# First attention of a two-layer transformer: the projections read raw transposed rows instead of rows that were normalized and transposed on the chip

## The reference, cut to what matters

```python
def _layernorm(x, axis=-1, eps=1e-05):
    m = jnp.mean(x, axis=axis, keepdims=True)
    v = jnp.var(x, axis=axis, keepdims=True)
    return (x - m) / jnp.sqrt(v + eps)
...
x = L0_attn_x                                   # 8 x 512 x 128
x = x + _L0_attn_ref(_layernorm(x), Wq, Wk, Wv, g_scale)
...
q = (x @ Wq.T)   # of the normalized rows; k and v in the same way
q, k = q / |q|, k / |k|  per head;  softmax(g_scale * q k^T) v
```

## Time and profile before

| what | us |
|---|---|
| timed runs: median of 3 (lowest to highest) | 1465.96 (1461.98 to 1473.85) |
| the profiled execution, its own time | 1452.33 |
| its span from first to last instruction | 1450.6 |
| busy in that span: PE / DVE / ACT / POOL | 1281.0 / 952.6 / 858.0 / 607.1 |
| mean granted clock of TensorE, of full speed | 0.960 |

### The profile page before, as it was taken

The page is one execution under the profiler, slowest core; times in us unless marked ns, Lnnn a source line. Parts: engine busy times, 40 slices in busy tenths (PEclk is TensorE's granted clock), DMA queues, the critical chain, the costliest instruction groups (busy, mean ns, idle before and its releaser), DMA issues.

```text
span 1450.6 us, 28493 instructions
## 1 busy us (share of the span) xinstructions
PE 1281.0 (88%) x9302; PEld 790.0 (54%) x9302; DVE 952.6 (66%) x3308; ACT 858.0 (59%) x1679; POOL 607.1 (42%) x783
## 2 busy tenths in 40 slices
PE   3877899999999999999999999998888886989982
PEld 1223455555555555555555555555555554878872
DVE  4475665677677766767676776656665762776784
ACT  3766666676666766675666676654534542555563
POOL 1000133342444435442533453345435444657674
PEclk8979999999999999999999999999989998999996
DMA  8041290000000000000000000001010001142422
GB/s 339 1 187 71 9 5 1 1 9 1 8 9 16 8 2 16 8 9 1 23 2 8 7 11 1 8 9 66 8 73 16 1 8 41 53 115 70 129 65 92
DMA packets 65455, 54.68 MB, mean 38 GB/s; under 512 B 41016, under 2 KB 51648, under 8 KB 65056
## 3 DMA queue, kind: packets, MB, share of 16 engines
q1 hardware_dynamic: 60768, 43.48, 14.0%
q0 software_dynamic: 4544, 9.38, 1.9%
HBM read 21.03 MB, written 31.81 MB: 36 GB/s over the span
## 4 chain that ended last, share of the span: by engine, by line
PE 61%; DVE 17%; ACT 10%; issue 7%; POOL 2%; POOLq 1%; DMA 0%; ACTq 0%; SPq 0%; DVEq 0%
PE scores L1745 11%; PE outs L1763 9%; PE outs L1889 7%; PE work L1685 7%; PE work L1792 4%; DVE scores L1238 3%; PE scores L1876 3%; DVE ra L1231 3%; ACT a_buf L947 3%; ACT ra L953 3%; PE outs L1968 2%; PE scores L1714 2%; PE work L1692 2%; PE work L1851 1%; PE work L1802 1%
## 5 line engine op out<-in xcount | busy, mean ns | idle before, releaser
L1238 DVE CUSTOM_DVE_ANT_0 scores<-scores,mask_qk 128x512 f32<-128x512 f32 (+3 forms) x512 | 238.8, 518 | 148.7 <-PE scores L1714 148.7
L941 ACT ACTIVATE big<-scores 128x1024 f32<-128x1024 f32 (+1 forms) x192 | 169.8, 885 | 214.3 <-PE scores L1745 214.2
L786 POOL TENSOR_SCALAR_AFFINE_SELECT big<-big 128x256 f32<-128x256 f32 x256 | 101.6, 410 | 461.0 <-ACT big L941 436.3
L947 ACT ACTIVATE a_buf<-scores 128x1024 f32<-128x1024 f32 x256 | 248.0, 1028 | 44.1 <-PE scores L1876 43.9
L1745 PE MATMUL scores<-ra 64*128 64x512 f32 (+3 forms) x1536 | 184.1, 345 | 10.6 <-ACT a_buf L947 4.7
L806 POOL TENSOR_TENSOR big<-big 128x768 f32<-128x768 f32 x64 | 116.8, 1824 | 136.2 <-issue 53.3
L1763 PE MATMUL outs<-big 128*64 128x512 f32 (+3 forms) x1024 | 156.9, 450 | 0.0
L1745 PEld LDWEIGHTS scores<-ra 64*128 64x128 f32 x1536 | 121.5, 187 | 61.7 <-issue 41.5
L1231 DVE TENSOR_TENSOR ra<-work,ra 128x512 fp32r<-128x512 f32 x128 | 88.3, 690 | 89.4 <-ACT ra L953 89.4
L1889 PE MATMUL outs<-a_buf 128*16 128x512 f32 x1024 | 143.8, 637 | 1.5 <-ACT a_buf L947 1.4
L1022 ACT ACTIVATE big<-scores,b_sb 128x128 f32<-128x128 f32 x312 | 89.4, 370 | 76.2 <-PE scores L1956 75.2
(11 more groups left out here) (223 smaller groups left out, 2540.5 us busy)
## 6 DMA issues: line engine op xcount, KB each, us to landing
sorted_rows<-xrows SPq DMA_DIRECT2D x34, 520.0 KB, 6.9
qkT<-sorted_rows SPq DMA_DIRECT2D x78, 65.0 KB, 1.8
a_buf<-in_w SPq DMA_DIRECT2D x2, 2048.0 KB, 7.9
a_buf<-in_x SPq DMA_DIRECT2D x8, 256.0 KB, 2.7
x_rows<-x SPq DMA_DIRECT2D x8, 256.0 KB, 2.0
ra<-x_rows SPq DMA_DIRECT2D x8, 256.0 KB
a_buf<-choice_rows SPq DMA_DIRECT2D x6, 256.0 KB, 3.9
yT<-choice_rows SPq DMA_DIRECT2D x5, 256.0 KB, 2.7
```

The costliest lines, as they stand in the source:

```text
L941: activation(prob1(g, i), d[:, :, 0:256] if i == 2 else d, ACT.Exp, scale=SCALE1).then_inc(unit_free("pair", g, i), 1)
L947: activation(prob0(c)[:, i * 1024:(i + 1) * 1024], unit_wait(act, "cosine", c, i), ACT.Exp).then_inc(unit_free("cosine", c, i), 1)
L1238: return v.tensor_tensor_reduce(scores_, scores_, mask_qk[:, SEQ - width:SEQ], -1.0, 3e38, ALU.add, ALU.min, neg_max[:, qt, j:j + 1])
```

## The change

The host hands over a second copy of the input, `x_T0`, with each batch transposed (128 numbers by 512 rows). SP loads it straight into `xT_h`, batch after batch, with one DMA of 256 KB each, which waits until the projections of the batch before were issued to the end. The standardizing instructions, the transposes, their copy, and the buffer `rows_h` go away, and POOL's wait for `rows_ready["a0"]` at `p = 3` with them.

The mean of a row is taken out by the weights: with W the weights by input, `(x - mean(x)) W = x (W - column mean of W)`. Once, at the start, PE sums the columns of the three weights with a matrix of ones (two matmuls, one for each half of the partitions of a bank), and DVE adds -1/128 of the sums to the weights. The factor `rstd` of a row, which is a row of the projection's result too, is applied by ACT when it moves the result: the two copies per tile become two activations that read a scale for each partition. The variances stay where they were, and use the second slot of their small buffers.

```diff
@@ work_order
     if p == 4:
         add(f, ("y0", f, 0), ("y0", f, 1))
-        add(h, ("xT0", h))
@@ SP
+            def next_x_T(h):
+                if h:
+                    work_wait(sp, "qkv0", h - 1, TILES - 1)
+                sp.dma_start(xT_h, x_T0[h]).then_inc(x_T_loaded, 16)
+
             sp.dma_start(x_in(0), x[0]).then_inc(x_loaded[0], 16)
             for dst, src in ((wqkv0_sb[:], wqkv0), (g_sb[:], g_scale.to_broadcast([P, 1]))):
                 sp.dma_start(dst, src).then_inc(first_in, 16)
+            next_x_T(0)
...
             for n in range(FILLS // 2):
                 zero_fill(n)
 
+            next_x_T(1)
+
             def next_x(h):
                 sp.wait_ge(x_taken, h - 1)
                 sp.dma_start(x_in(h), x[h]).then_inc(x_loaded[h % 2], 16)
+                next_x_T(h)
@@ POOL
-                if p == 3 and h is not None:
-                    pool.wait_ge(rows_ready["a0"], h + 1)
...
-                    inverse_deviations("a0", h)
+                    inverse_deviations("a0", h, 1)
@@ ACT
                 w = work_wait(act, "qkv0", h, t)
-                copy(qk0(h).rearrange("p (w t n) -> p w t n", w=2, t=TILES)[:, :, t, :],
-                     w[:, 0:2 * DIM].rearrange("p (w n) -> p w n", w=2))
-                copy(vstat(h)[:, t, :, 0:D0],
-                     w[:, 2 * DIM:3 * DIM].rearrange("p (h d) -> p h d", d=D0)
-                     ).then_inc(free_of("qkv0", h, t), 1)
+                act.wait_ge(rstd_ready["a0"], h + 1)
+                activation(qk0(h).rearrange("p (w t n) -> p w t n", w=2, t=TILES)[:, :, t, :],
+                           w[:, 0:2 * DIM].rearrange("p (w n) -> p w n", w=2), ACT.Copy,
+                           scale=rstd[:, 1, t:t + 1])
+                activation(vstat(h)[:, t, :, 0:D0],
+                           w[:, 2 * DIM:3 * DIM].rearrange("p (h d) -> p h d", d=D0), ACT.Copy,
+                           scale=rstd[:, 1, t:t + 1]).then_inc(free_of("qkv0", h, t), 1)
...
-                if p == 4 and h is not None:
-                    moved(xT_h, "xT0", h)
@@ DVE
             dve.wait_ge(first_in, 16 * 2)
+            dve.wait_ge(sums_full, 1)
+            v.scalar_tensor_tensor(wqkv0_sb[:], outs[:, 0, 0:3 * DIM], -1.0 / DIM, wqkv0_sb[:],
+                                   ALU.mult, ALU.add).then_inc(weights_centred, 1)
...
-                    variances("a0", x_in(h))
+                    variances("a0", x_in(h), 1)
...
-                if p == 3 and h is not None:
-                    standardize("a0", h, x_in(h), rows_h)
@@ PE
             pe.wait_ge(first_in, 16 * 2)
+            pe.wait_ge(consts, 1)
+            pe.wait_ge(out_free[1], 1)
+            for j in range(2):
+                last = mm(outs[j * D1:(j + 1) * D1, 0, 0:3 * DIM], ones[:], wqkv0_sb[:], start=True,
+                          stop=True)
+            last.then_inc(sums_full, 1)
...
                 if t == 0:
-                    work_moved(pe, "xT0", h)
+                    pe.wait_ge(weights_centred, 1)
+                    pe.wait_ge(x_T_loaded, 16 * (h + 1))
...
-                if p == 4 and h is not None:
-                    pe.wait_ge(rows_ready["a0"], h + 1)
-                    transposes(rows_h, "xT0", h)
```

More of the change, by code:

```diff
@@ L256 @@
 X_IN = VSTAT + 2 * TILES * H0 * VCOLS
-ROWS_H = X_IN + 2 * SEQ
-XT_H = ROWS_H + SEQ
+XT_H = X_IN + 2 * SEQ
 NORMS = XT_H + SEQ
@@ L278, with layers_kernel @@
 SPARSE = FINISH + EARLY.last * SEQ
-def layers_kernel(nc, x, wqkv0, g_scale, wg0, s0, bias_ln0, w1_0, b1_0, w2_0, b2_0,
+def layers_kernel(nc, x, x_T0, wqkv0, g_scale, wg0, s0, bias_ln0, w1_0, b1_0, w2_0, b2_0,
                   wq1, wk1, wv1, wo1, wg1, bg1, w1_1, b1_1, w2_1, b2_1, gamma, beta,
@@ L398, in layers_kernel @@
         xT_a, xT_b = a0_part(XT_A, SEQ), a0_part(XT_B, SEQ)
-        rows_h = rows_of(a0_part(ROWS_H, SEQ))
         xT_h = a0_part(XT_H, SEQ)
@@ L501, in layers_kernel @@
         x_loaded = [sem(f"x_loaded{i}") for i in range(2)]
+        x_T_loaded = sem("x_T_loaded")
+        sums_full = sem("sums_full")
+        weights_centred = sem("weights_centred")
         x_taken = sem("x_taken")
@@ L2135 @@
         "x": np.asarray(L0_attn_x).reshape(BATCH, TILES, P, DIM).transpose(0, 2, 1, 3),
+        "x_T0": np.asarray(L0_attn_x).transpose(0, 2, 1),
         "wqkv0": np.concatenate([np.asarray(w).T for w in (L0_attn_Wq, L0_attn_Wk, L0_attn_Wv)], 1),
```

## The result

| | before | after | ratio (95% interval) |
|---|---|---|---|
| 13 timed runs each, median (lowest to highest) | 1465.08 (1461.98 to 1473.85) | 1458.81 (1449.99 to 1460.58) | 0.9942 (0.9922 to 0.9961) |
| repeated on a second chip (A) | 1463.29 | 1451.85 | 0.9921 (0.9893 to 0.9949) |
| repeated on a third chip (C) | 1452.73 | 1444.59 | 0.9934 (0.9910 to 0.9959) |

The ratios are those of the mean times, not of the medians. The change makes the kernel faster by 0.6 to 0.8%, which is 8.5 to 11.6 us by the ratios; forecast were 5.6. By the medians it is 6.3 us in the first group, 11.4 on chip A and 8.1 on chip C. What the host spends on the transposed copy of the input is in none of these times. The profiled execution of the changed kernel took 1458.13 us, more than the 1452.33 of before's. What that is worth is the first thing the experiments had to settle.

A forecast was written before the change was run, and what follows sets the result against it. PE was taken to bound the steady passes. Steady passes -2.75, pass -1 -0.4, pass -2 0 and the start -2.5 sum to -5.6 us, from a median of 1465.96 to 1460.3 us, range 1451 to 1470.

The forecast's parts named there:

- Transposes, 0.59 us per pass: Passes 0 to 4, boundary of steps 4 and 5: PE loses four transposes, 0.59 us each pass, 2.95 us in all.
- The standardizing by DVE: End of step 3, 1.09 us: claimed to be in no steady chain, since PE has work from other stages meanwhile.
- Scaled copies: ACT's eight copies per batch cost about 0.10 us more each; 0.2 us in all reaches the steady passes.
- Rival B: ACT's scaled copies in step 5 of seven passes cost more than PE gains: +5.3 us, 1471.3 us; chance 0.06.
- Start and passes -3 to -1, -2.9 us: Before pass 0: -2.5 us from an earlier last copy of batch 0, 0 in pass -2, -0.4 in pass -1.
- pass -2: Step 5, nearly bound by ACT: the transposes' gain and the scaled copies' cost cancel, 0 us (bounds -0.6 and +0.6).
- pass -1: Step 5, chain through ACT's exponentials: PE 0.59 us earlier, tile 1's copies 0.2 more, -0.4 us (bounds -0.6 and 0).
- DMA 0: Transfers of the transposed input arrive in time and cost 0; 2.7 us if one came late by a whole landing.
- POOL's guard 0: Step 3: POOL's sums start some 4 us earlier at cost 0; otherwise 5 x 1.4 = 7 us of DVE.
- Rival A: DVE takes the transposes' place in steady passes: gain 0.23 us each, 1.15 in place of 2.75; 1462.0 us; chance 0.14.
- Rival D: The start is not shortened, since DVE's list waits for PE and the norm is 2.2 us later; 1462.8 us; chance 0.10.
- Rival C: PE's clock before pass 0 rises sooner or falls, -/+ 3.5 us: 1456.9 or 1463.9 us; chance 0.15 for both signs.

The follow-up runs named there:

- before_noguard: The kernel before without POOL's wait for the standardized rows at step 3; ratio to before 1.0045 (1.0027 to 1.0064), chip A.
- before_again: The kernel before, unchanged, run once more on chip A for a second trace and a null comparison; ratio to before 0.9997 (0.9978 to 1.0017).
- rows_kept_guard: The changed kernel with the unread standardizing by DVE and POOL's guard put back; ratio to before 0.9958 (0.9939 to 0.9977), chip B.
- rows_kept: The changed kernel, but DVE still writes the standardized rows that nobody reads, without POOL's guard; ratio to before 1.0053 (1.0029 to 1.0076), chip B.
- after: The changed kernel in its first group of runs and first trace; median 1458.81 us, ratio to before 0.9942 (0.9922 to 0.9961).
- after_again: The changed kernel, unchanged, run once more on chip A; ratio to before 0.9921 (0.9893 to 0.9949).
- after_third: The changed kernel, unchanged, run a third time on chip C as control; median 1444.59 us, ratio to before 0.9934 (0.9910 to 0.9959).
- guard_back: The changed kernel with POOL's row sums of step 3 held back again until the end of DVE's step 3; ratio to before 0.9936 (0.9914 to 0.9959), chip A.
- one_xT: The changed kernel, loading the transposed rows of batch 0 alone and using them for all batches; ratio to before 0.9944 (0.9920 to 0.9968), chip C.

## Why the prediction was right, point by point

1460.3 us was forecast, 1458.81 measured. The direction held, and so did the mechanism of every term that was priced; one term was missing. The gain was forecast at 5.6 us, and the ratios give 8.5 to 11.6. That the time came within 1.5 us is in part luck: in this group the medians differ by only 6.3 us, in the two repeated groups by 11.4 and 8.1.

- **Transposes, 0.59 us per pass**: 0.57. The places where I said the time would be made up (DVE's 1.37, ACT's 0.83) show it to 0.01 us in pass 3 of the first trace.
- **"The standardizing by DVE ... is in no steady chain"**: this is the step that failed. It held the score bank for 0.21 to 0.27 us by the periods (0.25 by the row), 1.0 to 1.4 us in five passes. I had put this term at 0, and it makes the steady gain 0.84 us per pass where 0.55 was forecast. The chain of waits leads through PE there, since a wait this short inside a group of four products of the same line doesn't show as one (the 1.20 us of before_noguard do); the row's length, 0.80 us in the first trace of before (0.79 in before_again) in place of 0.5, would have.
- **Scaled copies**: 0.09 us each, 0.10 forecast; nothing that shows in place of 0.2 us in the steady passes. Rival B is out.
- **Start and passes -3 to -1, -2.9 us**: the first exponential of pass 0 moved from 161.68 and 161.35 to 159.93, 156.69 and 158.99: -1.4 to -5.0, on average -3.0. The average fits, but the three differ by as much as the gain, and rows_kept_guard, which starts like the change, came only at 162.98. The last copy was forecast at 16.4 and came at 15.5 or 16.85. Whether pass -2 is really at 0 and pass -1 at -0.4 the traces can't tell, since the clock moves more than that.
- **DMA 0, POOL's guard 0**: both right. The 1.4 us per pass that I priced for POOL beside DVE is real, in the kernel that keeps the standardizing; that it did not come here because the one instruction of that kind at this place goes is what rows_kept shows, which keeps it.
- **Rival A** is out: DVE still waits 1.00 us. **Rival D** is out: POOL's power did end 2.4 us later, and the start was shorter all the same. **Rival C** is no rival but a band: kernels whose lists up to pass 0 are those of the change or nearly so (after, after_again, after_third, guard_back, rows_kept_guard, one_xT) reach pass 0 between 156.7 and 163.0 us.

From the first trace of before to after_third the account is: -2.7 to pass 0, -4.2 in passes 0 to 4, -1.5 for a fall of the clock in pass 3 of before that after_third did not have, and +0.9 from there to the end, together the -7.5 us between the spans of 1450.6 and 1443.1. The ratios give 1 to 4 us more, which their intervals cover, that of chip A only just (7.5 to 15.7 us). Whether the change also makes a fall of the clock rarer stays open: in passes 1 to 4 each of the three traces of before and before_noguard has one, and those of the change have two, none and none. The mean granted clock of the timed runs on chip A, 0.956 before and 0.966 after, can't settle it, because in some traces of the changed program, after_third among them, the granted clock reads 1.00 at the start where PE's instructions take the time of the lower level.

## What to carry to other kernels

Before two traces are compared, take a second trace of one of them: a wait of 1 us that recurs in four passes can belong to the group of runs in which that trace was taken, and not to the change. A wait without data behind it, like POOL's guard, may go only together with the instruction it protects; left in, it cost nothing that shows. And look for a hidden wait inside a group of like instructions by its length against the same group elsewhere.

## What the runs showed of the hardware

- DVE's subtract-and-multiply from SBUF to SBUF (128x128, fp32) waits while POOL adds in SBUF: in before_noguard 1.32 us in place of 0.33, ending 0.09 us after POOL's.
- A wait of PE of 1.81 us in an otherwise full stretch was followed by the lower clock in four of four passes (periods 3.3 to 3.9 us longer than the change's, rows_kept); in before_noguard, with 1.20 us at the same place, the clock stayed up there in all of them.
- ACT starts on PE's result 1.0 to 1.3 us late at one place of passes 2 to 5, in all four traces of one chip of three and in the change's first trace, for before, the change and two variants alike. DVE is late at the same place: in pass 4 of the change's first trace ACT starts at 713.79 and DVE at 713.85. POOL issues four indirect transfers just before, from 708.01 to 712.79, but it does so at the same place in before's first trace and in after_third, which have no lag; the cause was not tested.
- The granted clock in a trace can read 1.00 at the start of the program while PE runs at the time of the lower level: sixteen products took 3.62 us at a reading of 1.00 (after_third, 29.91 us) and at one of 0.50 (the change's first trace, 28.87 us).
